# The second layer's LSTM cells at steps 2 to 5 by seven block products in place of eight

## What is computed

```python
def step(carry, xt):
    h, c = carry
    g = xt @ Wih.T + h @ Whh.T + bias
    i, f, gg, o = jnp.split(g, 4, axis=-1)
    c = jax.nn.sigmoid(f) * c + jax.nn.sigmoid(i) * jnp.tanh(gg)
    h = jax.nn.sigmoid(o) * jnp.tanh(c)
    return ((h, c), h)
...
h = _lstm_layer(x, Wih0, Whh0, bih0, bhh0)
h = _lstm_layer(h, Wih1, Whh1, bih1, bhh1)
last = h[:, -1, :]
return ((last @ W1 + b1) @ W2 + b2) @ W3 + b3
```

## Time and profile before

| | |
|---|---|
| median of 3 runs | 1087.14 us (1083.89 to 1088.05) |
| the profiled execution | 1084.5 us, of which the span from first to last instruction is 1082.7 us |
| mean granted TensorE clock | 0.995 |
| TensorE, VectorE, ScalarE, GpSimd busy | 98%, 69%, 48%, 30% of the span |

### The profile page before, as it was taken

How to read it: one execution, slowest core, us unless ns; L and a number is a source line. 1 busy time by engine, 2 the same in 40 slices (tenths; PEclk the granted TensorE clock), 3 DMA queues, 4 the chain that set the end, 5 groups by cost and what they waited for, 6 DMA issues and landing times.

```text
span 1082.7 us, 14388 instructions
## 1 busy us (share of the span) xinstructions
PE 1062.1 (98%) x4905; PEld 507.6 (47%) x4905; DVE 742.7 (69%) x1155; ACT 517.3 (48%) x757; POOL 327.9 (30%) x353
## 2 busy tenths in 40 slices
PE   8799999999999999999999999999999999999998
PEld 6444444444445444444445444444444544444445
DVE  6589956666767866666867866567676775666554
ACT  3466444454555444434554544345554544444433
POOL 7650155624420056533440045552450000000000
PEclk9899999999999999999999999999999999999999
DMA  9310100000101100000011010000010110000001
GB/s 260 79 22 4 31 3 3 2 1 2 31 2 40 25 9 3 2 2 1 10 24 40 1 34 2 2 2 1 2 31 1 40 30 1 1 0 1 1 1 39
DMA packets 32082, 21.26 MB, mean 20 GB/s; under 512 B 19629, under 2 KB 25865, under 8 KB 32019
## 3 DMA queue, kind: packets, MB, share of 16 engines
q1 hardware_dynamic: 21223, 19.25, 6.2%
q0 software_dynamic: 9984, 1.12, 2.9%
q10 hardware_dynamic: 812, 0.07, 0.1%
HBM read 9.92 MB, written 4.19 MB: 13 GB/s over the span
## 4 chain that ended last, share of the span: by engine, by line
PE 90%; DVE 4%; issue 2%; ACT 2%; SPq 1%; another core or an unknown queue 1%; DMA 1%; DVEq 0%; ACTq 0%
PE acc L1518 51%; PE acc L1509 28%; PE acc L1503 5%; PE aux L1742 2%; SPq L496 1%; PE acc L1573 1%; PE acc L1582 1%; DVE gates L1143 1%; PE aux L1470 1%; PE aux L1464 1%; DMA w_nat<-in_L_rec_Wih 1%; DVE row_max L973 0%; DVE h_full L1190 0%; DVE h_part L1191 0%
## 5 line engine op out<-in xcount | busy, mean ns | idle before, releaser
L1518 PE MATMUL acc<-h_part,wh 128*128 128x512 f16 (+1 forms) x2640 | 644.2, 380 | 0.0
L1518 PEld LDWEIGHTS acc<-h_part,wh 128*128 128x128 f16 x2640 | 240.3, 98 | 314.5 <-issue 55.2
L1509 PE MATMUL acc<-h_part,wh 128*128 128x512 f16 (+1 forms) x1440 | 346.8, 379 | 0.0
L836 ACT ACTIVATE gates<-acc,gate_bias,unscale 128x512 f32<-128x512 f32 x246 | 189.7, 778 | 300.0 <-PE acc L1518 259.9
L836 ACT ACTIVATE gates<-gates,gate_bias,unscale 128x512 f32<-128x512 f32 x242 | 188.8, 810 | 144.9 <-DVE gates L1143 133.1
L1509 PEld LDWEIGHTS acc<-h_part,wh 128*128 128x128 f16 x1440 | 139.9, 98 | 171.8 <-issue 6.8
L653 POOL DMA_INDIRECT feat<-in_L_rec_region_tbl,region_idx x160 | 161.1, 1007 | 163.8 <-PE acc L1518 125.2
L1143 DVE TENSOR_TENSOR gates<-acc,emb_gates 128x512 f32<-128x512 f32 x242 | 160.5, 686 | 46.9 <-PE acc L1518 37.4
L653 POOL DMA_INDIRECT feat<-in_L_rec_poi_tbl,poi_idx x120 | 122.2, 1018 | 110.1 <-PE acc L1518 92.5
L1503 PE MATMUL acc<-x_in,wx 96*128 96x512 f32 (+1 forms) x242 | 135.0, 564 | 1.4 <-DVE gates L1143 0.7
L1190 DVE TENSOR_TENSOR h_full<-gates,tanh_c 128x512 f32<-128x512 f32 x120 | 82.8, 690 | 72.6 <-ACT tanh_c L841 66.9
(11 more groups left out here) (182 smaller groups left out, 418.8 us busy)
## 6 DMA issues: line engine op xcount, KB each, us to landing
out<-y SPq DMA_DIRECT2D x16, 256.0 KB, 2.1
x_in<-conv_hi SPq DMA_DIRECT2D x56, 64.0 KB, 2.0
feat<-in_L_rec_region_tbl,region_idx POOLq DMA_INDIRECT x160
w<-in_L_rec_W SPq DMA_DIRECT2D x4, 512.0 KB, 5.4
w_nat<-in_L_rec_Whh SPq DMA_DIRECT2D x2, 1024.0 KB, 8.8
w<-in_L_rec_W SPq DMA_DIRECT2D x1, 2048.0 KB
feat<-in_L_rec_poi_tbl,poi_idx POOLq DMA_INDIRECT x120
x_in<-conv_lo SPq DMA_DIRECT2D x28, 64.0 KB, 2.0
```

The lines of the kernel that those rows point to most:

```text
L836: nc.scalar.activation(gates[layer][:, j, g, :], source, ACT.Tanh if g == GATE_G else ACT.Sigmoid, bias=gate_bias[:, layer, m:m + 1], scal ...
L1509: mm = nc.tensor.matmul(bank, wh[:, 1, a, c, rows], h_part[0][:, s.write_slot, b, c, :], start=(c == 0 and a == b == HI), stop=(s.first an ...
L1518: mm = nc.tensor.matmul(bank, wh[:, own_w, a, c, rows], h_part[layer][:, s.read_slot, b, c, :], start=False, stop=(c == HK - 1 and a == LO))
```

## The change

The four gates' weights of the upper layer form, for each source, a matrix of 2 by 2 blocks: output tile `j` by contraction tile `c`. The moving h forms one too: contraction tile `c` by the left or right 256 columns. Before, the eight block products are made in four tiles' matmuls. The change makes seven (Strassen's scheme in Winograd's form), for the upper cells at steps 2 to 5 of each batch, 16 cells in all.

- The sums of weight blocks (`w_form`, four for each source, again HI and LO) are made once, by GpSimd in `weight_forms`, behind the first batch's last gather.
- The sums of h blocks (`t_full`, four of 128x256) are made for each step and each layer by VectorE (`t_forms`, three operations), their high part by ScalarE (`put_t_hi`), their low part by VectorE (`t_low`).
- `fast_cell` on TensorE is 14 products of 12 matmuls with 256 columns: the seven, for the gates i, g and for f, o. They use `acc` and the banks 1 and 3 of `aux`. Between them ScalarE copies six half sums (`part_copy`) and VectorE adds four (`part_sums`), and ScalarE takes the gates in quarters of 128x256.
- Around these cells VectorE handles both `j` in one operation of 128x1024 (`both_ig`, `both_fc`, `both_c`, `both_h`, `both_lo`); h's high part is a copy by ScalarE (`put_h_hi`). The tail of an upper cell (from f by c on) is done during the next lower cell, and the lower cell's update during the upper cell that follows.
- In all other cells the high part is a copy of `h_full` in place of a second product. tanh(c) is put where gate i was.
- The opening cell takes its banks in another order and a fifth one from `aux`; VectorE adds two of its tiles, then finishes the state that the upper cell left, then adds the rest. The third part of the embedding products moves behind the first tile of the following cell.
- The scale of the weights is four times smaller; `wx_rep`, `b3_row` and others move in memory.

```diff
+        low = lower(last_t - 1, fast(last_t - 3))
+        yield low
         if following:
             yield "turn", n + 1, 0
             yield "turn_emb", n + 1
-        yield cell(base, 1, last_t - 2, bank, (0, base.tile(last_t)))
-        yield cell(base, 0, last_t, bank, (1, base.tile(last_t - 1)))
+        end = fast(last_t - 2)
+        yield "upper", end, low[1]
+        low = lower(last_t, end)
+        yield low
+        yield "rest", low[1]
...
+            def weight_forms(w):
...
+                def combine(out, in0, in1, op):
+                    nonlocal done
+                    nc.gpsimd.tensor_tensor(out, in0, in1, op).then_inc(form_step, 1)
+                    done += 1
+                    pool.wait_ge(form_step, steps + done)
+                def whole(out, c, j):
+                    combine(out, block(HI, c, j), block(LO, c, j), ALU.add)
+                def put(k, value):
+                    hi, lo = flat(w_form[:, w, HI, k, :]), flat(w_form[:, w, LO, k, :])
+                    nc.gpsimd.tensor_copy(hi, value).then_inc(form_step, 1)
+                    nonlocal done
+                    done += 1
+                    pool.wait_ge(form_step, steps + done)
+                    nc.gpsimd.tensor_tensor(lo, value, hi, ALU.subtract).then_inc(forms_ready, 1)
...
+                whole(first, 0, 1)
+                whole(second, 1, 1)
+                combine(total, first, second, ALU.add)
+                put(0, total)
+                whole(second, 0, 0)
+                pool.wait_ge(forms_ready, w * FORMS + 1)
+                combine(total, total, second, ALU.subtract)
+                put(1, total)
+                combine(second, second, first, ALU.subtract)
+                put(2, second)
+                whole(first, 1, 0)
+                pool.wait_ge(forms_ready, w * FORMS + 2)
+                combine(first, first, total, ALU.subtract)
+                put(3, first)
...
+                    weight_forms(0)
+                    weight_forms(1)
...
+            def lower_acts(s, tail, plain_tail):
...
+                    act.wait_ge(part_acc, steps + 14)
+                    quarter(tail, 1, GATE_F, LEFT, half_bank(A2, 0), count=True)
+                    quarter(tail, 0, GATE_O, RIGHT, gates[1][:, 0, GATE_O, RIGHT], count=True)
+                    quarter(tail, 1, GATE_O, LEFT, half_bank(A2, 1), count=True)
+                gate_act0(s, 0, GATE_I)
+                if tail is not None:
+                    tanh_both(tail)
+                gate_act0(s, 0, GATE_G)
+                gate_act0(s, 0, GATE_F)
+                if tail is not None:
+                    put_h_hi(tail)
+                forms = tail if tail is not None else plain_tail
+                if forms.forms is not None:
+                    put_t_hi(forms)
...
+            def upper_acts(s, low):
...
+                for bank, source, step in ((B1, A1, 1), (B2, A2, 2)):
+                    act.wait_ge(part_acc, steps + step)
+                    nc.scalar.copy(bank, source).then_inc(part_copy, 1)
+                for bank, pair, step in ((B1, (GATE_I, GATE_G), 3), (B2, (GATE_F, GATE_O), 4)):
+                    act.wait_ge(part_acc, steps + step)
+                    for a, g in enumerate(pair):
+                        quarter(s, 0, g, LEFT, half_bank(bank, a))
+                tanh_both(low)
+                act.wait_ge(part_acc, steps + 5)
+                nc.scalar.copy(gates[1][:, 1, PAIR_A, RIGHT], gate_pair(E1)).then_inc(part_copy, 1)
+                act.wait_ge(part_acc, steps + 6)
+                nc.scalar.copy(gates[1][:, 0, PAIR_A, RIGHT], gate_pair(A1)).then_inc(part_copy, 1)
+                put_h_hi(low)
+                act.wait_ge(part_acc, steps + 7)
+                nc.scalar.copy(gates[1][:, 1, PAIR_B, RIGHT], gate_pair(E2)).then_inc(part_copy, 1)
...
+                act.wait_ge(part_acc, steps + 12)
+                for a, g in enumerate((GATE_I, GATE_G)):
+                    quarter(s, 1, g, LEFT, half_bank(A1, a), count=True)
...
-                nc.vector.tensor_tensor(hi, o_gate, th, ALU.mult).then_inc(h_hi_done[layer], 1)
                 dve.wait_ge(h_full_done[layer], split + 1)
+                nc.vector.tensor_copy(hi, h_full[:, j, :]).then_inc(h_hi_done[layer], 1)
...
-                    sums(s, 0)
+                    sums(s, 0, 0, 2)
                     if s.left is not None:
                         update_h(s.left, 1, 1)
+                    sums(s, 0, 2)
...
+            def t_forms(s):
...
+                nc.vector.tensor_tensor(t_full[:, 0:2, :], h4[:, 1:4:2, :], h4[:, 0:2, :], ALU.subtract
+                                        ).then_inc(t_step[layer], 1)
+                dve.wait_ge(t_step[layer], e * 3 + 1)
+                nc.vector.tensor_tensor(t_full[:, 2, :], h4[:, 3, :], t_full[:, 0, :], ALU.subtract
+                                        ).then_inc(t_step[layer], 1)
+                dve.wait_ge(t_step[layer], e * 3 + 2)
+                nc.vector.tensor_tensor(t_full[:, 3, :], h4[:, 2, :], t_full[:, 2, :], ALU.subtract
+                                        ).then_inc(t_step[layer], 1)
+            def t_low(s):
+                layer = s.layer
+                parts = (t_part1 if layer else t_part0[:, s.write_slot, :, :, :])
+                dve.wait_ge(t_hi_done[layer], s.forms + 1)
+                nc.vector.tensor_tensor(parts[:, LO, :, :], t_full[:, :, :], parts[:, HI, :, :], ALU.subtract
+                                        ).then_inc(t_done[layer], 1)
...
+            def lower(s, tail, plain_tail):
+                places = [(j, g) for j in range(HK) for g in s.gates]
+                if tail is not None:
+                    both_fc(tail)
+                    add_embeddings(s, *places[0])
+                    both_c(tail)
+                    add_embeddings(s, *places[1])
+                    add_embeddings(s, *places[2])
+                    both_h(tail)
+                    if tail.forms is not None:
+                        t_forms(tail)
+                    both_lo(tail)
+                    add_embeddings(s, *places[3])
+                    add_embeddings(s, *places[4])
+                    if tail.forms is not None:
+                        t_low(tail)
+                    for place in places[5:]:
+                        add_embeddings(s, *place)
...
+            def upper(s, low):
+                both_ig(low)
+                both_fc(low)
+                both_c(low)
+                both_h(low)
+                if low.forms is not None:
+                    t_forms(low)
+                both_lo(low)
+                part_sums(s, 0)
+                if low.forms is not None:
+                    t_low(low)
+                for k in range(1, ADDS7):
+                    part_sums(s, k)
+                both_ig(s)
...
+            t_forms(fourth)
...
+            t_low(fourth)
...
+                            pe.wait_ge(gate_sum, s.after_spread + SPREAD_FREE[place])
...
+            def fast_cell(s, low):
...
+                def product(bank, pair, left, right, opens, paces=False):
+                    for a, g in enumerate(pair):
+                        cols = slice(a * HALF, (a + 1) * HALF)
+                        for layer in range(2):
+                            for w, x in ((HI, HI), (HI, LO), (LO, HI)):
+                                mm = nc.tensor.matmul(bank[:, cols], weights(left, layer, w, g),
+                                                      moving(right, layer, x),
+                                                      start=(opens and a == layer == 0 and w == x == HI),
+                                                      stop=(a == layer == 1 and w == LO),
+                                                      skip_group_check=not opens)
+                        if a == 0 and paces:
+                            mm.then_inc(gate_acc[1], 1)
+                    mm.then_inc(part_acc, 1)
...
+                product(A1, FIRST_PAIR, A11, B11, True, True)
+                product(A2, SECOND_PAIR, A11, B11, True, True)
+                pe.wait_ge(part_copy, copies + 1)
+                product(B1, FIRST_PAIR, A12, B21, False, True)
+                pe.wait_ge(part_copy, copies + 2)
+                product(B2, SECOND_PAIR, A12, B21, False, True)
+                pe.wait_ge(gate_sum, low.tile + 7)
+                pe.wait_ge(t_done[0], s.fast + 1)
+                pe.wait_ge(t_done[1], s.fast + 1)
+                pe.wait_ge(forms_ready, 2 * FORMS)
+                product(E1, FIRST_PAIR, S1, T1, True, True)
+                product(A1, FIRST_PAIR, S2, T2, False, True)
+                pe.wait_ge(gate_sum, low.tile + 8)
+                product(E2, SECOND_PAIR, S1, T1, True, True)
+                pe.wait_ge(part_copy, copies + 3)
+                product(E1, FIRST_PAIR, S4, B22, False, True)
+                product(A2, SECOND_PAIR, S2, T2, False)
+                pe.wait_ge(part_copy, copies + 4)
```

(9 more changed lines are left out.)

336 lines of the change are left out of this document (303 added, 33 removed).

## The result

The changed kernel took 1113.06 us (median of 4 runs, 1111.98 to 1114.28) beside 1087.35 us for the kernel before: 1.0238 times as long, 95% interval 1.0215 to 1.0261. Forecast was 1075 us, 1054 to 1090. Its profiled execution has a span of 1112.5 us against 1082.7, +29.8.

A forecast was written before the change was run, and what follows sets the result against it. TensorE, busy 1062 of 1082.7 us, was taken as the bound. Terms: -38.1+4.9+2.6-3.0+22 = -11.6 us, so 1072.9 against the profiled 1084.5, median about 1075; range 1054 to 1090.

The forecast's parts named there:

- The saving: Seven-product cells: 168 matmuls at 0.1092 us in place of 96 at 0.2158, 2.38 us a cell, 38.1 for 16.
- The wait at product 3: Seven-product cell: TensorE waits 0.4 us for ScalarE's copy of product 1, queued behind gates; 12 cells, +4.9 us.
- After that each wait is met: Products 8 to 14 of a pair: inputs ready before TensorE needs them, for instance product 8 at 20.7, starting at 21.9.
- The steps: Step-by-step schedule of a pair of cells, 0.2 us until another engine sees a result; ends at 31.1 us, against 33.05.
- wrong if: Conditions refuting the forecast: form ops slower or running freely beside VectorE, bank-to-bank copy above 0.59 us, waits lowering the clock.
- ScalarE becomes the bound: Rival: copies for products 3, 8, 11 late behind 34 passes, each paying 0.2 us hand-over; 1100.7 us, chance 0.15.
- The weight forms: First batch's start: GpSimd's two-input passes (1.2 us) and casts (0.68) collide with VectorE's two-SBUF-input passes, TensorE waits; +22 us.
- End of a batch: After the lower cell at step 7, ScalarE's first gate of upper cell 6 is 0.85 us late; three batches, +2.6 us.
- Opening cells: Five banks and moved embedding products save about 1.0 us of TensorE's waits for VectorE's adds, three times: -3.0 us.
- VectorE's 26.0 us a pair: VectorE's work in a changed pair of cells, 14.6+9.7+1.7 = 26.0 us, said to fit into 31 us.
- The copy from bank to bank: ScalarE's copies of products into banks that later products want: no row existed, 0.59 us taken for each.

The follow-up runs named there:

- loud: Sessions in which the kernel before takes about 1087 us; the changed kernel took 1113.06 us there (1.0238).
- quiet: Sessions in which the kernel before takes about 1079 us; the changed kernel took 1058.8 us in one of them.
- the fills: Changed kernel with GpSimd's 32 weight-form passes replaced by 8 fills of the same buffers with zeros: 1099.7 us (1.0142), in a later session 1096.6 us (1.0075).

## Why the prediction was wrong, point by point

The span in two parts, at the first cell of seven products (before: the upper cell in its place):

```
                              forecast   loud                          quiet
start to the cell at step 2     +22      158.26 - 139.34 = +18.9       148.49 - 133.44 = +15.1
from there to the end          -33.6     954.2 - 943.4  = +10.9        908.3 - 943.4  = -35.1
sum                            -11.6     +29.8                         -20.0
```

- **The saving: right.** 256-column matmuls 0.109 apart, a cell of 18.26 to 18.49 where nothing stalls.
- **The wait at product 3, +4.9: the step that failed.** "TensorE waits 0.4. After that each wait is met." Quiet it was close to that: 0.1 to 0.2 in the cells at steps 2 to 4, 0.7 at step 5, 3.7 in all. Loud it was 49.6, ten times the term, in cells that the steps had as met. The steps counted 0.2 us until another engine sees a result, everywhere. Loud and beside gathers TensorE's signals took 3 to 4 us, and with margins of 0.35 to 3.0 us at products 8 to 14 they reach TensorE. The kernel before has nearly as many gathers, but fewer of its increments lie beside three or more (105, not 227), fewer of those are late (9, not 95), and its eight tiles in four banks may hide them; I didn't separate the three. The last of my "wrong if" came true on top: the granted clock is 0.95 over the stalled pair, with stretches at half rate (1.2 GHz) behind the waits, and 1.00 in the other pairs.
- **The rival "ScalarE becomes the bound"** had the right place, the copies wanted by products 3, 8 and 11, and a hand-over price as its mechanism, but on each pass and always. ScalarE does 23.5 us in a pair, not 25.2, in 36 passes (I had written 34 for the same list); it wasn't the bound. That its time, 1100.7, is nearer to the loud one than mine is luck: its price lay on ScalarE, the real one on TensorE's signals.
- **The weight forms, +22: the collision is real, its size was off and a part of the cost was another.** Removing them gave 15.7 of 18.9 us; 2.5 of the rest lie before the second cell (71.92 for 69.45). From the second cell to the cell at step 2 the start grew by 16.4 loud and 16.0 quiet. I had priced some 21 as TensorE's waits. In the quiet trace its waits there sum to 10.7 us (1.5 of them for a gather), and the granted clock, 1.00 in the kernel before, lay at the half level for 10.2 us behind them, where six matmuls take 2.56 us in place of 1.295:

```profile
119.16 2.05 PE L1815 MATMUL aux<-head_sum,one_col 128*128 128x512 f32 x2 [4.41 <-DVE head_sum L1296]
121.00 2.77 PE L1898 MATMUL acc<-h_part,wh 128*128 128x512 f16 x6
123.56 1.93 PE L1907 MATMUL acc<-h_part,wh 128*128 128x512 f16 x6
```

  That is some 4 us, my estimate from these rows and TensorE's busy part of the 10.2 us; my sum had nothing for the clock, only the "wrong if". With the fills the clock stayed at 1.00. So waits half as long as priced, and a clock not priced, came to a figure near mine by luck. GpSimd's two-input passes took 1.4 to 1.5 us on average (1.2 to 1.7 by form), not 1.2, and most casts 0.89, not 0.68; VectorE's passes beside them 1.1 to 1.5 us, not 1.7. Its casts from SBUF went from 0.51 to 0.84 (quiet); passes that read a bank kept their 0.68. By the Trainium skill ("SBUF — State Buffer", section on the two separate sides) the shared port pair is locked for whole instructions, against passes with two SBUF inputs and VectorE's fast modes; the rows agree in which passes pay.
- **End of a batch, +2.6:** +0.1 each, not 0.85. **Opening cells, -3.0:** -0.7 each, 24.46 to 23.77, so -2.1. **VectorE's 26.0 us a pair:** 24.6. **The copy from bank to bank:** 0.57 us, 0.59 taken.

**Open.** What makes a session loud. Three marks go together: the kernel before is 5.9 us later, all of it before its second cell (69.45 for 63.54); fewer increments are recorded for each gather (6 to 10 of 16); TensorE's are late. Missing records and late signals at the same time may mean one path that both share and that has less room then; no run shows it, and VectorE's and ScalarE's signals, on time throughout, speak for something of TensorE's own. All executions here were recorded by the profiler, so whether the recording itself makes the signals late wasn't separated; that rival stands. The Trainium skill ("Perfetto Trace Analysis", in its table of a TensorE instruction's stages) says that a matmul's end is estimated and that its signal is pushed once PSUM has acknowledged the write; by that the delay could also lie in the write. No run here tells these two apart.

## What to carry to other kernels

A schedule whose engines hand over every 1.3 us lives off the signal's delay: price that delay beside the densest traffic of the kernel, not only where it is quiet, and look where gathers run densest. Thinning them there is what the counts point to; no run of mine showed it as a cure. Measure a change again in another session, and look at the kernel before first: when its own time has moved, two experiments from different sessions can't be compared. Work on GpSimd with two SBUF inputs is paid by VectorE's two-input passes beside it, so put it where VectorE reads banks or idles, and count the granted clock behind TensorE's waits as part of the price.

## What was not expected of the hardware

- TensorE's increments recorded 4 to 9 us apart, 12 and 28 us late, with VectorE idle and TensorE nearly so, while GpSimd issued gathers 1.25 us apart (167.47, 171.67, 180.74, 189.15).
- 16.0 increments recorded for a gather when quiet; loud 10.2 in the kernel before, 7.6 in the changed one, 6.1 where the gathers were densest, but also 6.4 where most were left out.
- Only TensorE's signals came late to those who waited: 50 of 315, and 0 of 336 of VectorE's and ScalarE's.
- A single-input pass on GpSimd lengthens VectorE's two-input passes as well, to 0.83 and 0.92 us on average.
